# AdaLN block with selective scan and ternary FFN: new side-work slots, gate sign in the weights, last states by DMA

## The reference

```python
mod = (_silu(L0_c) @ L0_wmod).reshape(L0_c.shape[0], 6, 1, -1)
sa, ca, ga, sb, cb, gb = (mod[:, 0], ..., mod[:, 5])
ga = (2 * (ga >= 0) - 1) * jnp.maximum(jnp.abs(ga), 0.25)      # gb alike
h = _layernorm(x) * (1 + ca) + sa
x = x + ga * ssm(h)
h = _layernorm(x) * (1 + cb) + sb
x = x + gb * ffn(h)
# ssm(x), 256 channels, 16 states, 2048 tokens
dt, B_in, C_in = split(x @ x_proj_w.T, [128, 144])
delta = softplus(dt @ dt_proj_w.T + dt_proj_b); A = -exp(A_log)
h = exp(dt_t[..., None] * A) * h + dt_t[..., None] * B_t[:, None, :] * x_t[..., None]   # token by token
y_t = einsum('bdn,bn->bd', h, C_t) + D_param * x_t
# ffn(x), 704 hidden, ternary weights
out = ((silu(x @ gate_w.T * gate_s) * (x @ up_w.T * up_s)) @ down_w.T) * down_s
```

## Time and profile before

| what | value |
|---|---|
| median of 3 runs | 392.27 us (392.23 to 397.02) |
| profiled execution | 390.5 us, span of its instructions 388.6 us |
| mean granted TensorE clock | 0.794 |
| busy share | PE 68%, DVE 67%, POOL 66%, PEld 51%, ACT 48% |

### The profile page before, as it was taken

The page is one execution under the profiler, slowest core; times in us unless marked ns, Lnnn a source line. Parts: engine busy times, 40 slices in busy tenths (PEclk is TensorE's granted clock), DMA queues, the critical chain, the costliest instruction groups (busy, mean ns, idle before and its releaser), DMA issues.

```text
span 388.6 us, 3720 instructions
## 1 busy us (share of the span) xinstructions
PE 265.9 (68%) x1190; PEld 196.3 (51%) x1190; DVE 258.9 (67%) x340; ACT 185.4 (48%) x318; POOL 257.1 (66%) x146
## 2 busy tenths in 40 slices
PE   8910947744576658737799369475993693775996
PEld 8600834333453536526567156263772472554774
DVE  3136499899269868789595965598969445970221
ACT  2546425743436585973454826832247168205320
POOL 2038799999984899999158699983586972213000
PEclk9975587855568887888699768867996679598999
DMA  8359971143544141341022965230139200000001
GB/s 294 117 117 307 166 167 69 41 111 113 97 104 93 31 93 63 117 100 42 0 48 72 148 147 110 71 90 1 44 80 173 58 2 0 0 0 29 27 0 57
DMA packets 20117, 33.03 MB, mean 85 GB/s; under 512 B 1856, under 2 KB 7168, under 8 KB 20096
## 3 DMA queue, kind: packets, MB, share of 16 engines
q1 hardware_dynamic: 19680, 31.95, 34.5%
q10 hardware_dynamic: 416, 0.81, 0.6%
HBM read 30.40 MB, written 2.36 MB: 84 GB/s over the span
## 4 chain that ended last, share of the span: by engine, by line
POOL 29%; PE 26%; issue 14%; DVE 13%; ACT 11%; DMA 3%; SPq 2%; DVEq 0%; POOLq 0%; ACTq 0%
POOL drv L546 16%; POOL drv L559 7%; PE side L1055 6%; DVE state L861 6%; PE sums L1133 5%; DVE drv L842 4%; ACT decay L719 3%; DMA brow<-bc_dram 3%; PE side L1088 3%; PE side L1010 2%; ACT gates L701 2%; POOL h_lo L506 2%; PE rows_ps L1107 1%; PE decay L1072 1%; PE side L1072 1%
## 5 line engine op out<-in xcount | busy, mean ns | idle before, releaser
L546 POOL TENSOR_TENSOR drv<-u,brow 128x1024 f32<-128x1024 f32 x64 | 153.4, 2411 | 12.9 <-DMA brow<-bc_dram 12.7
L861 DVE TENSOR_TENSOR_SCAN state<-decay,last,drv 128x512 f32<-128x512 f32 x96 | 121.3, 1274 | 44.9 <-ACT decay L719 44.8
L1133 PE MATMUL sums<-ident,drv 128*128 128x128 f32 x512 | 89.1, 332 | 54.7 <-POOL drv L559 46.2
L719 ACT ACTIVATE decay<-delta,A 128x512 f32<-128x512 f32 x128 | 87.5, 685 | 70.4 <-DVE state L861 68.0
L1133 PEld LDWEIGHTS sums<-ident,drv 128*128 128x128 f32 x512 | 72.3, 171 | 73.2 <-POOL drv L559 52.8
L559 POOL TENSOR_TENSOR drv<-state,crow 128x1024 f32<-128x1024 f32 x28 | 66.1, 2360 | 33.3 <-DVE state L861 33.2
L1107 PE MATMUL rows_ps<-c_parts,sel 64*128 64x512 f32 x36 | 22.7, 631 | 58.2 <-DVE drv L842 54.2
L842 DVE TENSOR_TENSOR drv<-state,rows_ps 128x512 f32<-128x512 f32 x72 | 47.6, 662 | 1.6 <-PE rows_ps L1107 1.6
L861 DVE TENSOR_TENSOR_SCAN state<-decay,drv 128x512 f32<-128x512 f32 x32 | 38.5, 1214 | 14.4 <-ACT decay L719 9.2
L1107 PEld LDWEIGHTS rows_ps<-c_parts,sel 64*128 64x128 f32 x36 | 8.3, 229 | 71.6 <-DVE drv L842 61.5
L1088 PE MATMUL side<-down_sb,gates 128*128 128x256 f32 x120 | 31.6, 414 | 2.5 <-ACT h L637 2.5
(11 more groups left out here) (127 smaller groups left out, 321.5 us busy)
## 6 DMA issues: line engine op xcount, KB each, us to landing
brow<-bc_dram SPq DMA_DIRECT2D x32, 512.0 KB, 5.6
crow<-bc_dram SPq DMA_DIRECT2D x12, 512.0 KB, 7.9
resid<-in_x SPq DMA_DIRECT2D x4, 512.0 KB, 6.6
out<-resid SPq DMA_DIRECT2D x8, 256.0 KB, 2.1
crow<-bc_dram SPq DMA_DIRECT2D x4, 256.0 KB, 8.8
gates<-in_wmod ACTq DMA_DIRECT2D x1, 768.0 KB, 5.8
gates<-in_wmod SPq DMA_DIRECT2D x1, 768.0 KB, 7.1
ffn_sb<-in_gateT SPq DMA_DIRECT2D x1, 640.0 KB, 6.7
```

Of the source, the lines that this page charges most:

```text
L546: nc.gpsimd.tensor_tensor(drv[j % RING_DRV][:, :, 0:S], u[:, c % 2, :, 0:S], b.unsqueeze(1).to_broadcast([P, HALVES, S]), ALU.mult).then_i ...
L719: nc.scalar.activation(decay[i % RING_DECAY][:, 0:S], delta[:, c % 2, h, 0:S], ACT.Exp, scale=A[:, h * N + n:h * N + n + 1]).then_inc(deca ...
L861: nc.vector.tensor_tensor_scan(state[j % RING_STATE][:, h, 0:S], decay[i % RING_DECAY][:, 0:S], drv[j % RING_DRV][:, h, 0:S], before, ALU. ...
L1133: ins = nc.tensor.matmul(sums[:, b * D + h * P:b * D + (h + 1) * P], of[:, h, b * P:(b + 1) * P], ident[:, :], is_transpose=True, start=Fa ...
```

## The change

It has seven parts.

1. Places: nearly all side tasks move by half a slot to two slots; on TensorE the additions stand behind the side work and the row, ADD_LAG is 3, and states 13 to 15 are added in slot 16. `up3`, `up4`, `hdn2` to `hdn4` and `down` now lie in the next step. GpSimd takes its side work first in a slot. LEAD is 3, the ring `drv` has 12 buffers. Banks change with it.
2. The last states are copied by DMA from SBUF to SBUF on SyncE's queue: 48 DMAs of 128 x 2 words, one semaphore per state buffer. The scan that reuses the buffer, four states later, waits for the copy.
3. `hmod` is made once, times the sign of the gate. The sign goes into `W_sb` and `xbc_sb` too, |gate| into delta, A, D and the bias. `hmodg` goes (eight activations).
4. The FFN's shift is folded: `h2T` is only scaled, and a bias `wb` = weights times shift (22 short matmuls, one setup) is added at `gates` and `hdn`. `up_s` goes into `down_sb` (six activations on ScalarE in step 0).
5. `h2_lo` is made on VectorE, from PSUM, in two instructions. The activations that wrote `h2` go.
6. SyncE's loads stand one slot earlier; in the setup the second brow load stands ahead of the weights of the FFN.
7. The setup task `W` stands behind `mod` on VectorE.

```diff
 PLAN = {
     "vector": [
-        (16, "K hdn4"), (1.5, "K x2"), (2, "K st0"), (2.5, "K st1"), (18.5, "K out0"), (3, "K agg"), (20, "K out1"),
+        (17.5, "K hdn4"), (1.5, "K x2"), (2, "K st0"), (2.5, "K st1"), (2.5, "K agg"), (19, "K out0"), (21, "K out1"),
+        (7.5, "K lo0"), (8, "K lo1"), (8.5, "F clo"), (9.5, "F delta0"), (10.5, "F delta1"),
...
     "gpsimd": [
-        (3, "K rstd"), (4, "F cap"), (7, "K lo"), (9, "F u"), (-3, "F rstd"),
+        (4, "K rstd"), (6, "F cap"), (11, "F u"), (-2, "F rstd"),
...
     "scalar": [
-        (-2, "F xn0"), (-1.5, "F xn1"), (0.5, "F hmod0"), (1, "F hmod1"), (1.5, "F hmodg0"), (2, "F hmodg1"),
+        (-0.5, "F xn0"), (0, "F xn1"), (2.5, "F hmod0"), (3, "F hmod1"), (4.5, "F exp0"), (4.5, "F zb0"),
...
-LEAD = 4
-ADD_LAG = 2
+LEAD = 3
+ADD_LAG = 3
-RING_DRV = 10
+RING_DRV = 12
 def add_slot(n):
-    return 3 if n == 0 else N if n >= N - 2 else n + ADD_LAG
+    return min(n + ADD_LAG, N)
...
+            def keep_last(c, n):
+                sp.wait_ge(scan_done, upto_scan(c, n, HALVES - 1))
+                sp.dma_start(last[:, n, :], state[(c * N + n) % RING_STATE][:, :, CHUNK[c] - 1],
+                             allow_slow_non_contiguous=True).then_inc(upto_kept(c, n)[0], 16)
             for step in steps:
                 for slot in range(N):
+                    if 0 <= step < NCH - 1:
+                        keep_last(step, slot)
...
-                elif name == "lo":
-                    nc.gpsimd.tensor_tensor(h2_lo[:, :, 0:S], h2[:, :, 0:S], h2_hi[:, :, 0:S].bitcast(F32),
-                                            ALU.subtract).then_inc(h2_lo_ready, 1)
+                elif name in ("lo0", "lo1"):
+                    dve.wait_ge(h2_hi_ready, HALVES * c + h + 1)
+                    nc.vector.scalar_tensor_tensor(h2_lo[:, h, 0:S], src[:, 0:S], mod[:, 8 + h:9 + h],
+                                                   h2_hi[:, h, 0:S].bitcast(F32), ALU.mult, ALU.subtract)\
+                      .then_inc(side_free[i], 1)
...
-                        dve.wait_ge(last_kept, upto_kept(c - 1, n))
+                        dve.wait_ge(*upto_kept(c - 1, n))
...
                     if spread and not follows:
                         spread_row(step, n)
-                    for c, m in adds_at(step, n):
-                        add_state(c, m)
                     for task in side_tasks("tensor", step, n):
                         side_work(*task, full_weights)
                     if spread and follows:
                         spread_row(step, n)
+                    for c, m in adds_at(step, n):
+                        add_state(c, m)
```

203 lines of the change are left out of this document (117 added, 86 removed), and 37 rows, old and new, of tables (FIRST, PLACE, PLAN).

## The result

The changed kernel takes **361.27 us** in the median of 4 runs (359.98 to 365.03), the kernel before beside it 392.37 (392.23 to 397.02, 4 runs): a ratio of 0.920 with a 95% interval of 0.910 to 0.930. The profiled execution took 360.38 us, with a span of 358.5 and a mean granted clock of 0.819. The forecast was 364.0 us, 350 to 384.

A forecast was written before the change was run, and what follows sets the result against it. A chain of queues from GpSimd product to scan, over VectorE's work, was taken as the bound. Steps 278.5 against 311.4 (-32.9), head +1, tail +3.5 gave 362.1 profiled; with 1.8 for the median, 364 us, range 350 to 384.

The forecast's parts named there:

- (a): Step 0: VectorE's 7.12 us wait, through ScalarE, for chunk 2's layer norm factors goes; 7.6 us of idle time stays.
- (b): Start of steps 1 and 2: waits of 3.58 and 4.37 us behind `hmod`, which waited for `xT`, go.
- rival A: Waits only change places, TensorE is the next queue; 14 of the gates' 17.5 us stay: 378 us, chance 0.15.
- (c): Steps 2 and 3: VectorE's idle time put down to the gates, 7.5 and 10 us, all goes.
- (d): Steps 1 to 3: VectorE's wait during silu's table loads and activations, when no `decay` is made, stays at 4 us each.
- (e): In the steps: small VectorE waits where a side activation lands between two decays stay, 3 to 4.5 us a step.
- Rival C: With ScalarE lighter and TensorE at its upper clock, small waits and the `out1` wait go too: 350 us, chance 0.10.
- Rival B: The DMA copies of last states hold up scans, from 17 us a copy on; at 21 us, 405 us; chance 0.08.
- rival D: GpSimd bounds all steps, at about 75 us each, so little is gained: 388 us, chance 0.05.
- The signs: Right: VectorE idle 8 to 14 us in steps 1 to 3, clock over 0.81; wrong: GpSimd over 95% busy there.
- Head: Before the first scan: `z` starts later, the first drive stands behind less; +1 us (0 to +2).
- Tail: After the last product: residual begins at +2.8 us, down blocks at +7.4; 3.5 us longer in all.

The follow-up runs named there:

- e2: The kernel before with only TensorE's additions moved, one slot later, behind side work and row; 372.6 us, ratio 0.946.
- e8: The change with LEAD 4 instead of 3 and `F u` one slot earlier in GpSimd's queue; 361.2 us, ratio 0.921.
- e1: The change with TensorE's additions ahead of the side work again, at a lag of 2 slots; 375.5 us, ratio 0.960.
- e3: The change with gate 1 in gate 0's PSUM bank again; 370.1 us, ratio 0.935.
- e10: The kernel of e5 without the silu of chunks 0 to 2 and its table loads; 338.8 us, ratio 0.864.
- e7: The change plus 16 ScalarE activations of 128x512 from PSUM, of the kind it had removed; 366.3 us, ratio 0.932.
- e4: The change with the last states kept by 48 two-column ScalarE activations instead of DMA copies; 359.4 us, ratio 0.915.
- e11: The change with 10 `drv` buffers instead of 12; 361.0 us, ratio 0.912.
- e6: The change plus 28 and 16 unread TensorE transposes ahead of the tail's two pairs of down blocks; 358.8 us, ratio 0.914.
- e5: The change with chunk 2's FFN tasks, gate 0 to the second down blocks, one slot earlier on every engine; 350.4 us, ratio 0.893.

## Why the prediction was nearly right

**The bound: right.** I read the kernel as bounded by a chain of queues with VectorE's work under it, not by an engine. The gain lies where that says: VectorE's busy time per step stands still, its idle time in the steps fell from 72.0 to 30.4 us (271.1 less 240.7 of work), and e2 gets 20 us by moving nothing but TensorE's additions.

**Wait (a), step 0: the sum right, its two terms not.** The step took 70.0 us as summed, with the 7.6 us of idle time that I kept. But of the 7.12 us that were to go, 2.19 stayed, and the other waits of the step, 7.1 us before, fell to 5.4 where I had added 0.5 for the shorter lead; e8 shows that this term had the wrong sign. The two misses cancelled, which was luck.

**(b) and `out1`: right.** VectorE no longer waits behind `hmod` in steps 1 and 2, and waits 5.28 and 2.43 us for `out1` where I had 5 and 1.5. That is rival A's mechanism, at the place where TensorE was full. In step 1 it shows up too, unforeseen: VectorE waits 2.44 us for the additions of slot 16, which now stand together.

**(c) the gates: right, all gone.** ScalarE waits 2.2 us for them in all instead of 28.7, all of it in the tail, and VectorE never waits behind that in the steps. e1 and e3 show the two halves of the reason, the additions ahead of the gates and the shared bank (some 5 us).

**(d) silu: right**, 2.5, 3.7 and 3.8 us for 4 each; e10 prices it at 11.7 us in all.

**(e) the small waits: wrong, and the sum's first error.** I took them for side activations landing between two decays, and kept 4.3, 3.2 and 3.3 us. The small waits for `decay` vanished. What idle time is left beside silu and `out1` is 4.0 us in step 1, nearly all of it the two new waits for TensorE, and 0.8 and 0.4 us in steps 2 and 3: 5.2 us for 10.8. This and the shorter silu wait of step 1 (2.5 for 4) make up most of the 7.4 us by which steps 0 to 3 came out below 278.5. The sum did not follow its own count either: of step 2's 21.9 us idle, rows 2 and the 3.5 given to the gates leave 1.4 and not 3.2, of step 3's 20.7 there were 2.7 left and not 3.3, and in step 1 it lets 3.3 us go that no term names (15.2 idle, less 3.58, 4 and 4.3).

The trace of the kernel before shows what two of the small waits were. VectorE's 1.69 and 1.83 us in step 1 (at 137.69 and 140.79) stand behind these two activations, which waited for TensorE:

```profile
136.29 0.78 ACT L637 ACTIVATE h_hi<-side,mod 128x512 fp32r<-128x512 f32 x1 [3.23 <-PE side L1024]
...
139.12 0.59 ACT L644 ACTIVATE bc_sb<-side 32x512 f32<-32x512 f32 x1 [1.47 <-PE side L1010]
```

So ScalarE asked for inputs that TensorE had not made, as at the gates; in the change the same two tasks find theirs ready. Rival C had the small waits go because ScalarE became 6 us a step lighter and TensorE's clock rose. e7 speaks against the first reason, for with 16 of the activations back the steps don't change, and e4 with the other 48; no run has all of them back together. The second was not tested: the granted clock of step 1 was 0.76, below the 0.81 of the kernel before, and that of steps 2 and 3 above it. With the additions late and the places old (e2) small waits for `decay` are still there. That fits the new places as the cause but doesn't single them out, since e2 keeps the rest of the kernel before as well. Which of the moved tasks gave how much I haven't taken apart.

**Parts 2 to 5 in the steps: right as far as tested.** The copies cost nothing (e4), the lighter ScalarE gains nothing (e7), and `h2_lo` takes 741 ns, with none of the upper bound of 2.4 us more. Rival B's wait for a copy never came (13.3 us at most). What part 5 is worth on GpSimd no run shows. GpSimd was busy 64.5 of 65.2 us in step 1, so with the 2.35 us of `h2_lo` still there that step would need 66.9 us (my estimate, the sum of the two), and rival D was nearer than its 0.05 says. GpSimd busy over 95% was one of my signs of being wrong; it came, with 99% in step 1. Yet after the first scan of the change no wait of VectorE ended directly with GpSimd's work. It did so with LEAD 4 (e8), and through ScalarE in the 2.19 us of (a).

**The signs.** TensorE's waits for products went, and silu and `out1` are the longest waits, as said. Three signs of being right did not come as written: VectorE was idle 6.5, 9.8 and 6.6 us in steps 1 to 3 and not 8 to 14, the clock was over 0.81 in steps 2 and 3 only, and the first gate of the tail came at +30.3 and not at 22 to 24.

**Head: outside its range in the trace**, -0.7 us for +1 (0 to +2). `z` started 0.8 us later than before, and `u` on GpSimd 1.1 us later, but the first drive came 0.7 us earlier (29.63 for 30.32): the 1.8 us of layer norm factors that had stood ahead of it were gone, and I had named them without giving them a size of their own. The clock of `z`, which the sum leaves out, moves the head as much: of the ten traces with this head, three have `z` at the upper clock, as the kernel before had it, and the first scan at 32.1 to 32.3; the others have it at the lower one, six with the first scan at 33.8 to 34.2 and one at 35.3. So where the head falls inside the range, it is by the clock.

**Tail: the second error, +10.9 us for +3.5.** The step of the working that failed is "`up4` can start only after `hdn0` ... the residual begins at +2.8": I overlooked that `up3` stands ahead of `up4` and the addition of state 12 ahead of both, and that this addition could not begin before the row of state 15 had its bank. So the additions began 3.2 us after the last product, not before its end. The down blocks then began at +10.4 for +7.4 (3.0 us of the miss), and I priced both pairs at 6.0 us where they took 8.7 and 7.65 at the lower clock (4.35 us). Together 7.35 of the 7.4 us. The clock's share is as large as this only in some executions: in e8 and e11, with the same tail, the first gate came 2.6 us earlier. e6 gives the clock's share back, e5 the whole: with the work of chunk 2 a slot earlier the tail is 3.7 us shorter than that of the kernel before.

The two errors were of equal size, -7.4 and +7.4 us, and that they cancelled was luck; what is left of the profiled execution, 360.4 for 362.1, is the head's 1.7. The forecast's own range of 356 to 371 holds the first error alone (357) and just misses the second (371.4).
